# The weights' mean pass moved into the Q/K/V projection loops, and the second layernorm's x loads moved to POOL's queue

## What is computed

```python
mod = silu(c) @ wmod                      # six vectors of 1024: sa, ca, ga, sb, cb, gb
h = layernorm(x) * (1 + ca) + sa
x = x + ga * attention(h, W_qkv)          # 16 heads of 64, softmax over 2048 keys
h = layernorm(x) * (1 + cb) + sb
x = x + gb * ffn(h, w_gate, w_up, w_down) # 1024 -> 4096 -> 1024

def _weight_quant(w):                     # on each of the three FFN weights
    scale = 1.0 / clip(mean(abs(w)), 1e-05)
    return clip(round(w * scale), -1.0, 1.0) / scale
```

## Time and profile before

| | us |
|---|---|
| median of 2 runs | 4189.65 (4172.76 to 4206.54) |
| the profiled execution, its own time | 4174.14 |
| its span, slowest core | 4172.6 |
| spans of the 8 cores | 4149.2 to 4172.6 |
| busy in that span: PE, DVE, ACT, POOL | 2837.4, 1667.1, 1074.3, 243.1 |

### The profile page before, as it was taken

One profiled execution on the slowest core, in us unless ns is written; L12 is line 12 of the kernel. 1 busy time (PEld: TensorE's weight loads), 2 busy tenths in 40 slices (PEclk: granted clock), 3 DMA queues, 4 the chain that ended last, 5 costly groups with the idle time before them and its releaser, 6 DMA issues.

```text
span 4172.6 us, 29948 instructions; the slowest of 8 cores (4149.2 to 4172.6 us)
## 1 busy us (share of the span) xinstructions
PE 2837.4 (68%) x8156; PEld 777.1 (19%) x8156; DVE 1667.1 (40%) x2462; ACT 1074.3 (26%) x1183; POOL 243.1 (6%) x445
## 2 busy tenths in 40 slices
PE   7439302788888888888888888620176685785866
PEld 1114100111111111111111111100122231331322
DVE  0451563332233233323323323237756357246354
ACT  0101005322333233232323223211233234124132
POOL 0000000110111011011101101000000000000000
PEclk9769655566666666656666666655587796895987
DMA  5333580110111011111101101252231440531523
GB/s 203 125 94 43 204 279 1 51 46 25 44 46 46 23 46 46 29 39 46 46 23 46 46 24 45 69 151 81 91 118 56 130 130 23 169 114 46 164 74 99
DMA packets 210311, 331.58 MB, mean 79 GB/s; under 512 B 136113, under 2 KB 136370, under 8 KB 195810
## 3 DMA queue, kind: packets, MB, share of 16 engines
q1 hardware_dynamic: 168274, 235.27, 17.9%
q0 software_dynamic: 41872, 94.40, 8.5%
HBM read 289.68 MB, written 42.01 MB: 79 GB/s over the span
## 4 chain that ended last, share of the span: by engine, by line
PE 53%; DVE 25%; DMA 11%; ACT 5%; issue 4%; DVEq 1%; SPq 0%; ACTq 0%; POOL 0%; POOLq 0%
PE sps L725 12%; PE sps L718 12%; PE avps L762 5%; PE dops L766 5%; PE avps L758 4%; PE bcps L784 3%; DVE drow L776 3%; DVE drow L779 3%; PE dps L1370 2%; DVE gq L1302 2%; DVE vq L1329 2%; DMA xbb<-x 2%; DVE gpb L1206 2%; DVE gup L1219 2%; PE gps L1192 2%
## 5 line engine op out<-in xcount | busy, mean ns | idle before, releaser
L734 ACT ACTIVATE PT<-sps 128x1024 bf16<-128x1024 f32 x512 | 524.3, 1024 | 467.1 <-PE sps L725 467.0
L718 PE MATMUL sps<-c,onesb 1*128 1x512 bf16 x1024 | 524.1, 613 | 9.4 <-DMA c<-C8h 8.8
L725 PE MATMUL sps<-Qc,Kc 64*128 64x512 bf16 x1024 | 527.8, 617 | 0.0
L1192 PE MATMUL gps<-hA,tg 128*128 128x512 bf16 x1024 | 249.7, 387 | 191.7 <-DMA tu<-ternu 122.0
L779 DVE RECIPROCAL drow<-dops 1x512 f32<-1x512 f32 x32 | 107.1, 3346 | 638.1 <-PE dops L766 638.1
L776 DVE RECIPROCAL drow<-avps 1x512 f32<-1x512 f32 x32 | 107.3, 3352 | 416.8 <-PE avps L758 416.8
L788 ACT ACTIVATE bcsb<-bcps 128x512 bf16<-128x512 f32 x64 | 38.2, 597 | 914.2 <-PE bcps L784 914.2
L784 PE MATMUL bcps<-drow,onecf 1*128 1x512 f32 x128 | 109.6, 950 | 238.4 <-DVE drow L776 119.3
L762 PE MATMUL avps<-PT,Vc 128*64 128x512 bf16 x512 | 243.9, 476 | 21.1 <-ACT PT L734 21.1
L1196 PE MATMUL ups<-hA,tu 128*128 128x512 bf16 x1024 | 247.0, 385 | 0.0
L1315 PE MATMUL dps<-gq,td 128*128 128x512 bf16 x256 | 129.3, 608 | 160.8 <-DVE gq L1302 160.8
(11 more groups left out here) (169 smaller groups left out, 2687.9 us busy)
## 6 DMA issues: line engine op xcount, KB each, us to landing
tg<-terng SPq DMA_DIRECT2D x128, 256.0 KB, 2.8
tu<-ternu SPq DMA_DIRECT2D x128, 256.0 KB, 3.1
td<-ternd POOLq DMA_DIRECT2D x32, 1024.0 KB, 6.4
wmb<-wmod SPq DMA_DIRECT2D x8, 2048.0 KB, 8.9
xs<-xT SPq DMA_DIRECT2D x16, 1024.0 KB, 5.5
mb<-wgT SPq DMA_DIRECT2D x8, 2048.0 KB, 9.5
mb<-wuT SPq DMA_DIRECT2D x8, 2048.0 KB, 9.2
mb<-wdT SPq DMA_DIRECT2D x8, 2048.0 KB, 9.2
```

The source lines that it names most:

```text
L718: p.inc(TE.matmul(sps[sp][:, n2 * 512:(n2 + 1) * 512], onesb[0:1, :], cb[0:1, cs:cs + 512], start=True, stop=False), eT)
L725: p.inc(TE.matmul(sps[sp][:, n2 * 512:(n2 + 1) * 512], lhsT, Qc[bp:bp + 64, q0:q0 + 512], start=False, stop=True, tile_position=(bp, 0)), eT)
L734: p.inc(S.activation(PT[hb][:, kt * 1024:(kt + 1) * 1024], sps[sp], AF.Exp, scale=0.125), eS)
L1192: p.inc(TE.matmul(gps[pb], tgc[buf][:, d * 128:(d + 1) * 128], hA[:, d * T + ts0: d * T + ts0 + 512], start=(d == 0), stop=(d == NDC - 1)) ...
```

## The change

Four edits.

The mean pass becomes a function, `emit_mean_unit`, which emits one of the 24 pieces: SP's load and DVE's reduction. It is called at the end of each of the 16 passes of the Q/K loop and of every second pass of the V loop, 24 times in all. Its first call, after pass ec = 0, makes SP wait for h, and for what ACT and PE were given so far (with ec = 0 among it).

`wc0` and `wc1` move to the left side of SBUF, where nothing else lies at that time, and POOL's wait for h ahead of the first column load is gone. PE no longer waits for the whole of h; in pass ec = 0 it waits for slice d ahead of that slice's four matmuls (`lnap_tok[d]`). `mb0`, `mb1` and `macc` are allocated ahead of the loops, beside `wvt`.

In the second layernorm's statistics the loads of x are issued by POOL (queue q0, semaphores `dgx0`/`dgx1`) instead of SP, with the same waits. The stores to x2tmp stay on SP, the cast copies to xbb on POOL.

```diff
     def emit_ln_apply(src_dram, scale_vec, shift_vec, dest_tile, Rbo, MRbo,
-                      tok_rb, extra_wait_ds=False):
+                      tok_rb, dtoks=None):
...
+            if dtoks is not None:
+                dtoks[d] = p.cnt[eV]
...
-    g_wc0, wc0 = alloc("wc0", [128, 1024], BF16, "right")
-    g_wc1, wc1 = alloc("wc1", [128, 1024], BF16, "right")
+    g_wc0, wc0 = alloc("wc0", [128, 1024], BF16, "left")
+    g_wc1, wc1 = alloc("wc1", [128, 1024], BF16, "left")
...
+    def emit_mean_unit():
+        k = mean_state["k"]
...
+        if k == 0:
+            p.wait(Y, "Y", eV, tok_h)
+            p.wait(Y, "Y", eS)
+            p.wait(Y, "Y", eT)
...
+        buf = k % 2
+        if k >= 2:
+            sem_e, tok_e = red_tok[k - 2]
+            p.wait(Y, "Y", sem_e, tok_e)
...
+        tok_m = p.dma(Y, "Y", dns, outm, src)
+        dstc = macc[:, base + j:base + j + 1]
+        p.wait(V, "V", dns, tok_m)
+        p.wait(V, "V", eV)
+        p.inc(V.reduce_sum(dstc, mbuf[buf], axis=AXX,
+                           apply_absolute_value=True), eV)
+        red_tok[k] = (eV, p.cnt[eV])
+        mean_state["k"] = k + 1
...
         for ec in range(16):
             buf = ec % 2
-            if ec == 0:
-                p.wait(G, "G", eV, tok_h)
...
             p.wait(TE, "T", dqs, tok_w)
-            p.wait(TE, "T", eV, tok_h)
...
             for d in range(NDC):
+                if ec == 0:
+                    p.wait(TE, "T", eV, lnap_tok[d])
...
                 evac_tok[buf] = (eS, p.cnt[eS])
+            emit_mean_unit()
...
             vevac[buf] = p.cnt[eV]
+            if t % 2 == 0:
+                emit_mean_unit()
...
-            tok_xd = p.dma(Y, "Y", dxs, xsb[buf], xT[d * 128:(d + 1) * 128, :])
+            tok_xd = p.dma(G, "G", dxs, xsb[buf], xT[d * 128:(d + 1) * 128, :])
```

More of the change, by code:

```diff
@@ L383, in _build_nc_inner @@
     p.wait(V, "V", eV, tok_modvecs)
+    lnap_tok = {}
     tok_h = emit_ln_apply(xT, avec, modv[:, 0:8],
[L385 removed]
+                          lambda d: hA[:, d * T:(d + 1) * T], Rb, MRb, tok_rb,
+                          dtoks=lnap_tok)
     if KPHASE < 3:
@@ L404, in _build_nc_inner @@
     tok_vones = p.cnt[eV]
+    g_mb0, mb0 = alloc("mb0", [128, 4096], F32, "right")
+    g_mb1, mb1 = alloc("mb1", [128, 4096], F32, "right")
+    g_macc, macc = alloc("macc", [128, 24], F32, "right")
+    mbuf = [mb0, mb1]
+    mean_plan = []
+    for (wsrc, base) in [(wgT, 0), (wuT, 8), (wdT, 16)]:
+        for j in range(8):
+            mean_plan.append((wsrc, base, j))
+    mean_state = {"k": 0, "red": {}}
+    def emit_mean_unit():
+        k = mean_state["k"]
+        if k >= len(mean_plan):
+            return
+        wsrc, base, j = mean_plan[k]
+        red_tok = mean_state["red"]
+        if k == 0:
+            p.wait(Y, "Y", eV, tok_h)
+            p.wait(Y, "Y", eS)
+            p.wait(Y, "Y", eT)
+        if wsrc.shape[0] == D:
+            src = wsrc[j * 128:(j + 1) * 128, :]
+        else:
+            src = r3_in(wsrc[j * 512:(j + 1) * 512, :])
+        buf = k % 2
+        if k >= 2:
+            sem_e, tok_e = red_tok[k - 2]
+            p.wait(Y, "Y", sem_e, tok_e)
+        outm = mbuf[buf] if wsrc.shape[0] == D else r3_out(mbuf[buf], 4)
+        dns = "dn%d" % buf
+        tok_m = p.dma(Y, "Y", dns, outm, src)
[6 more added lines that the diff above has]
+        mean_state["k"] = k + 1
     with (nc.psum_tensor("qkpsA", [128, T], F32) as qa,
@@ L472, in _build_nc_inner @@
             vevac[buf] = p.cnt[eV]
+            if t % 2 == 0:
+                emit_mean_unit()
     tok_v = p.cnt[eV]
     g_wv.__exit__(None, None, None)
[L476 to L506, removed]
+    while mean_state["k"] < len(mean_plan):
+        emit_mean_unit()
     p.wait(V, "V", eG)
@@ L847, in _build_nc_inner @@
             buf = d % 2
-            dxs = "dx%d" % buf
+            dxs = "dgx%d" % buf
             if d == 0:
-                p.wait(Y, "Y", eG)
-                p.wait(Y, "Y", eT, tok_p3T)
+                p.wait(G, "G", eG)
+                p.wait(G, "G", eT, tok_p3T)
             if d >= 2:
-                p.wait(Y, "Y", eV, use_tok[(d - 2, "x2stt")])
-                p.wait(Y, "Y", eS, use_tok[(d - 2, "x2s")])
+                p.wait(G, "G", eV, use_tok[(d - 2, "x2stt")])
+                p.wait(G, "G", eS, use_tok[(d - 2, "x2s")])
                 p.wait(V, "V", "dsx%d" % buf, use_tok[(d - 2, "st")])
```

## The result

The changed kernel takes 4062.45 us (median; 4055.80 to 4102.65), the kernel before in the same rounds 4190.51 us (4172.76 to 4232.80). In the profiled execution of after, the cores of die 0 were granted less clock than in that of before; core 7, whose rows stand ahead, wasn't, so core 7 is compared here (0.691, before 0.682). The two medians lie 128 us apart, the two spans of core 7 114.4 us: the runs of the kernel before spread over 60 us, and the forecast was made against the profiled one of them, which is among the fastest.

The account below looks back on a forecast made before the run. PE bounded the Q/K stage, then DMA loads with latency the mean pass; merged, DMA time bounds the stage. 4174.1 - 141.4 (merge) + 21.7 (layernorm loads) + 2 (early column loads) = 4056.4, given as 4057 us, range 4018 to 4115.

Parts of the forecast that it names:

- the gain of the Q/K and V stage: Mean pass beside the Q/K and V matmuls: sums collected at 481.8 instead of 623.2, a gain of 141.4 us.
- The head: Start of Q/K: PE follows h slice by slice, so ec 0 is done at 268.3 instead of 281.4.
- The early column loads: Program start: two column loads take DMA time from the first wmod loads; 2 us charged, bounds 0 and 5.5.
- 8.83 us a step: Q/K loop: one mean load (6.06) and one column load (2.77) of DMA time per step, 14 steps, 123.6 us.
- C: Rival, Q/K loop: packets taken in turn, columns wait for four mean loads, 12 us a step, 4100 us; chance 0.20.
- A: The forecast itself, merged Q/K stage: DMA time bounds it, 4057 us, own range 4035 to 4085; chance 0.60.
- C's own signs: Q/K loop: waits of 15 us and more for wc, once in four steps, and reductions in bursts.
- reductions every 8 to 9 us: Sign that the forecast is right: DVE's reductions stand every 8 to 9 us in the Q/K stage.
- 10 x 7.00 us: V stage: the 10 mean loads left run at the pass's own pace, 70.0 us.
- 2.9 us a slice: Second layernorm: load last of three transfers on POOL, 12.3 us against 9.4, seven times, 20.3 us lost.
- The term for the first load: Second layernorm: the first x load on POOL's queue costs 6.4 us instead of 5.0.
- Rival B: Second layernorm: loads cost nothing on POOL, slipping in before the casting copy; 4035 us; chance 0.15.

Follow-up runs that it names:

- cols7_v: The changed kernel with seven column buffers, columns 1 to 6 loaded early, and PE's V loop waiting for the last cast, not the reductions behind it: 4032.64 us.
- pair3_act: The changed kernel with paired column loads in three buffers, V loop waiting for h alone, layernorm loads back on SP, all Q/K casts on ACT: 4030.49 us.
- cols7_late: The changed kernel with seven column buffers instead of two, columns 2 to 6 loaded only when h is complete: 4045.45 us (one run).
- cols4: The changed kernel with four single column buffers instead of two: 4048.24 us (one run).

## Why the prediction was right, and where three of its terms were not

The time was right to 5 us, by luck: the gain of the Q/K and V stage was put 19.4 us too high and the loss of the layernorm 14 us too high, and the two cancel. On core 7 the sum of the forecast, -141.4 + 21.7 + 2 = -117.7, stands beside -122.0 + 6.2 + 2.3 and -0.9 elsewhere = -114.4.

**The head.** ec 0 was to be done 1.9 us after h; PE's four last matmuls start at 268.93 and take 1.86. Right. The early column loads: h ends 2.3 us later on core 7, 0.4 later as a mean of die 1. In the six other runs with the same early loads it ended at 261.6 to 267.6 us (means of a die), 264.6 on average, against 262.3 before. That agrees with the 2 us, but on a spread of 6 us it doesn't show them.

**The Q/K loop: 8.83 us a step, mis-sized.** Forecast: column 15 landed at 268.3 + 2.9 + 123.6 = 394.8, its pass done at 401.7, 135.3 us after h. Measured 163.8 on core 7, 28.5 more (159.4 as a mean of die 1). What stands above the 15 passes of 6.91 us was put at 29.8 us, 2.9 of latency and 14 steps of 1.92. The trace has 44.5 us of waiting for columns (seven waits, above), 14.7 more, and six sets of matmuls of 8.08 to 9.71 us, which run at the lower of the two clocks for a while, together 13.5 more. Five of the six follow the waits for columns, the first follows the wait for h. A chain of DMA time presumes that the engines always have the work that is wanted next. The prices of the two loads held: over 268 to 403 us the shares of 60.7% and 25.4% are 6.0 us for each mean load and 2.9 for each column. The presumption didn't: the engines were at 86%, because with two buffers on either side each stream stopped when the other was late. "PE's gaps of 1.9 us a step shouldn't cost clock" was right for gaps of 1.9 us, and there were hardly any such gaps.

**The mechanism was C's, at about half of C's price.** I took from the earlier trace rows that whole transfers are served in the order in which they arrive. The 100 packets against 100, and the 225 against 228 with smaller ones, show turns. This is what the Trainium skill (DMA: Bandwidth & Descriptors, Queues, rings and completion order) says, and the trace agrees in that. A packet in the Trainium skill (the same section) holds several descriptors, while the profile counts single runs of 16 KB and 256 B, and equal counts over some microseconds don't show how many of these go at a turn.

The rows that I set against it show something else, a late start. In seven of the eight slices of the layernorm before, POOL's copy sent its first packet 6.1 to 6.5 us after its issue, behind some 240 packets of SP's store and load. In the eighth, issued at 2779.26, no load of SP's came between, and it started after 2.8 us (the DMA of the 4 us from its issue, kernel before):

```profile
q1 hardware_dynamic: 144, 1.05, 65.3%
q0 software_dynamic: 63, 0.26, 32.1%
```

So its packets would have been due. The Q/K stage has the same: a column load alone sends its first packet 1.6 us after its issue (before, from 281.99 on), and those issued at 271.34, 312.85, 350.35 and 390.54 in after, beside a mean load, after 4.2 to 5.6 us. Once both streams run they go in turns. Why the start is late no run shows.

C overstated the price: it let four mean loads follow each other before a column is through, while in fact SP's queue runs dry after one or two (two buffers, and each load waits for a reduction). Its count was off as well. 272 packets are the mean of two kinds of load, 144 for w_gate and w_up, which are those of the Q/K loop, and 528 for w_down. By turns alone, 66 against 9 an engine, a column would have outlasted seven mean loads, not four. So the step measured 10.5 us, (159.4 - 2) / 15, midway between A's 8.83 and C's 12. C's own signs, waits of 15 us and more once in four steps, came out as 6 to 12 us once in three or four. And "reductions every 8 to 9 us" was wrong: they came in pairs.

**The V stage: 10 x 7.00 us, too dear.** From the end of the Q/K loop to the sums 80.1 us were forecast and 71.0 measured. 16 of the 24 units, not 14, were done by 435.4, and the other 8 went at DVE's pace of 7.2 us. That the pace is close to the 7.00 of before is chance: the run with a quarter of the bytes has the same V loop. So -9.1 here and +28.5 above make the 19.4 us by which 141.4 was too high.

**The layernorm: 2.9 us a slice, mis-sized.** 0.9 on core 7, 0.7 as a mean of the cores, and 0.6 by putting it back. The sum took copy and load in a row as 0.5 + 5.9 + 6.4, each with its own time from issue to landing. But back to back they share that latency. (The copy also brings 0.5 MB, not 1.) The three together take (57.2 + 27.9)% of 9.5 us = 8.1 us of the engines, 2.7 each, and one latency. What is left of the edit is that the load is issued 0.6 us later and takes 0.2 us longer. The term for the first load was right: 6.35 us against 5.02, which stands in the row of attention above. The Trainium skill (DMA: Bandwidth & Descriptors, Issuing engines are not separate DMA queues) has only issue time to save by such an edit. The trace agrees for most of what a slice lost, 0.6 of 0.9 us; the 1.3 us of the first load aren't issue time. Rival B, which I gave 0.15, was nearer in size than the forecast, but not by its own mechanism: the load didn't slip in ahead of the copy, which had landed when PE used it at 2579.06, 3.4 us before the load. Had the Q/K and V term been right, the time would have been near 4042 us (4174.1 - 141.4 + 2 + 6.2 + 1.3).

**What was to stay the same** did: column norms -0.4, attention -1.9 us. The granted clock from 280 to 400 was 0.85 on core 7 and 0.89 on core 4, before 0.97 on core 7. A clock well under 0.9 was named as a sign against the forecast, and it was one: 13.5 us.

## What to carry to other kernels

When a stream of large packets is laid beside a stream of small ones, look whether the small one is held to equal counts, as here, and moves only in the gaps of the large one; give it buffers for the longest such stretch (here two column buffers lost 33 us of Q/K loop that four hid) before counting on the sum of both DMA times. Price transfers that run back to back by the time their packets take and one latency, not by their times to landing added up. When a wait is removed and the end stays (cols7_v, pair3_act), look part by part at which engine is full: in cols7_v it was DVE behind the Q/K loop, in pair3_act the DMA engines in the loop. A share over the whole stage (95.8%) hides that.

## What the runs showed of the hardware

Two queues that both have packets under way moved equal numbers of them, of 16 KB against 256 B (100 to 100) and of 4 KB against 256 B (225 to 228). A transfer of POOL's that was issued while SP's queue was full began late: first packet after 4.2 to 5.6 us instead of 1.6 for a column load, 6.1 to 6.5 instead of 2.8 for the layernorm's copy.

The end of a load can trail. The column load issued at 279.21 landed at 303.50, and from 298 to 302 only 12 of its packets went out, beside 106 of SP's. By equal turns 106 packets in 4 us are 1.7 a microsecond for each of 16 engines, so 3 a microsecond are the turns of two; an estimate, since the trace doesn't name the engine of a packet.

A load that is issued far ahead doesn't land soon: wvt took 17.3 us before, 51.9 with four column buffers and 70.7 in cols7_late (core 7). In cols7_late PE had other waits at that place, in cols4 it stood 17.3 us for wvt.

In the layernorm the same 432 packets of a slice took 9.4 us of the 16 engines before (56.6 + 21.7% of the 12 us from 2706) and 8.1 after. The 239 packets of SP's two transfers alone took 101.6% of 6 us. Why they took longer side by side wasn't tried and stays open.
